# A third weight grid, four patch places and the sums on GpSimd's queue in a deformable sampling stage

## The reference

```python
def _dcnv3_core(x, offset, mask):           # B, H, W, C, G = 4, 56, 56, 128, 16; K = 9; GC = 8
    px = gx + dx + off[..., 0]              # places of the nine taps
    py = gy + dy + off[..., 1]
    x0, y0 = floor(pxf), floor(pyf)
    for cx, cy in ((x0, y0), (x0 + 1, y0), (x0, y0 + 1), (x0 + 1, y0 + 1)):
        wgt = (1 - abs(pxf - cx)) * (1 - abs(pyf - cy))
        v = take_along_axis(xg, idx, axis=1)
        acc = acc + (wgt * valid)[..., None] * v
    out = (acc * mask).reshape(B, H * W, K, G, GC).sum(axis=2)
```

## Time and profile before

| | |
|---|---|
| median of three runs | 3215.72 us |
| profiled execution, its own time | 3216.21 us |
| its span | 3214.5 us |
| VectorE busy, whole span | 2227.2 us (69%) |
| TensorE busy, whole span | 2288.7 us (71%) |
| clearing of the grids on GpSimd | 64 memsets, 187.1 us in all, mean 2.92 us |
| loads of `deform_xw` | 112 of 504 KB |
| loads and stores of `deform_yt` | 4 and 4, of 1568 KB each, median 7.2 us to landing |

### The profile page before, as it was taken

The page is one execution under the profiler, slowest core; times in us unless marked ns, Lnnn a source line. Parts: engine busy times, 40 slices in busy tenths (PEclk is TensorE's granted clock), DMA queues, the critical chain, the costliest instruction groups (busy, mean ns, idle before and its releaser), DMA issues. The chain is left out here.

```text
span 3214.5 us, 46923 instructions
## 1 busy us (share of the span) xinstructions
PE 2288.7 (71%) x15979; PEld 1511.7 (47%) x15979; DVE 2227.2 (69%) x4935; ACT 1623.1 (50%) x3184; POOL 1042.7 (32%) x1059
## 2 busy tenths in 40 slices
PE   5999804655756656527749999999999994403996
PEld 3555403555655555414415455455445553401775
DVE  2888846889899898439957768767777755400776
ACT  1444326667676676224456755664764631101664
POOL 0455501222122222139912222222122222273555
PEclk9999956877778778667769999999999995556998
DMA  6477748657657453462230002001001003012221
GB/s 180 100 182 162 179 115 220 172 148 197 174 144 186 139 147 88 107 258 80 79 82 1 1 1 60 1 1 37 24 1 31 11 10 104 5 41 90 90 90 52
DMA packets 343238, 304.60 MB, mean 95 GB/s; under 512 B 73775, under 2 KB 299703, under 8 KB 341536
## 3 DMA queue, kind: packets, MB, share of 16 engines
q1 hardware_dynamic: 334208, 294.00, 33.3%
q0 software_dynamic: 8800, 7.70, 0.8%
HBM read 158.50 MB, written 156.80 MB: 98 GB/s over the span
## 5 line engine op out<-in xcount | busy, mean ns | idle before, releaser
L1913 ACT ACTIVATE attn_prob<-attn_ps_e,attn_nm 128x448 f32<-128x448 f32 (+1 forms) x700 | 438.7, 632 | 324.5 <-DVE attn_nm L2000 321.9
L1817 PE MATMUL attn_ps_r<-attn_prob,attn_xs 128*128 128x448 f32 (+1 forms) x1400 | 585.7, 548 | 5.0 <-POOL attn_xs L1719 5.0
L940 PE MATMUL deform_ps_w<-all_ident,deform_grid 128*126 128x128 f32 x1568 | 268.0, 337 | 316.3 <-DVE deform_grid L1025 199.9
L2000 DVE TENSOR_REDUCE attn_nm<-attn_ps_e 128x1 f32<-128x448 f32 (+1 forms) x700 | 407.7, 615 | 36.7 <-PE attn_ps_e L1805 34.7
L866 POOL MEMSET deform_grid<- 128x3752 f32 (+1 forms) x64 | 187.1, 2924 | 709.1 <-PE deform_ps_w L940 663.4
L1716 POOL TENSOR_TENSOR attn_xs<-attn_xa,attn_wz 128x381 f32<-128x381 f32 (+1 forms) x200 | 184.4, 946 | 715.8 <-DVE attn_wz L2021 715.8
L940 PEld LDWEIGHTS deform_ps_w<-all_ident,deform_grid 128*126 128x126 f32 x1568 | 231.6, 176 | 351.5 <-DVE deform_grid L1025 211.3
L1817 PEld LDWEIGHTS attn_ps_r<-attn_prob,attn_xs 128*128 128x128 f32 (+1 forms) x1400 | 263.5, 192 | 208.2 <-issue 176.8
L900 ACT ACTIVATE deform_wt<-deform_ps_w 126x896 f32<-126x896 f32 x224 | 203.5, 933 | 227.5 <-PE deform_ps_w L940 143.1
L885 ACT ACTIVATE deform_hat<-deform_rel,block_negr 128x504 f32<-128x504 f32 (+1 forms) x256 | 258.6, 1124 | 104.0 <-DVE deform_rel L985 103.7
L1025 DVE TENSOR_TENSOR deform_grid<-deform_grid,deform_prod 128x448 f32 (+1 forms) x512 | 297.8, 582 | 8.8 <-DVE deform_grid L1025 7.9
(11 more groups left out here) (321 smaller groups left out, 4131.1 us busy)
## 6 DMA issues: line engine op xcount, KB each, us to landing
deform_xw<-shifted SPq DMA_DIRECT2D x112, 504.0 KB
shifted<-deform_xm SPq DMA_DIRECT2D x8, 4032.0 KB, 12.4
offsets_masks<-offs_om SPq DMA_DIRECT2D x48, 378.0 KB
deform_om<-offsets_masks SPq DMA_DIRECT2D x48, 378.0 KB
dispatched<-rows_zero SPq DMA_DIRECT2D x1, 16512.0 KB, 48.7
experts_bi<-dispatched SPq DMA_DIRECT2D x32, 516.0 KB, 3.5
deform_xa<-projected SPq DMA_DIRECT2D x64, 168.0 KB
projected<-offs_zero SPq DMA_DIRECT2D x13, 680.0 KB
```

What stands on the lines that cost most here:

```text
L940: mm = pe.transpose(ps_w[n % 2][0:NPOS, q * LANES:(q + 1) * LANES], grid[:, u % 2, at:at + NPOS], ident[:, :])
L1817: mm = pe.matmul(ps_r[n % 2][:, 0:BK], xs[0:rows, at + i, j, :], prob[0:rows, at + i, j * BK:(j + 1) * BK], start=(i == 0), stop=(i == len ...
L1913: nc.scalar.activation(prob[0:rows, slab(S) + i, ch * BK:(ch + 1) * BK], ps_e[u % NE][0:rows, 0:BK], ACT.Exp, bias=nm[0:rows, S % 2, i, ch ...
L2000: nc.vector.tensor_reduce(nm[0:rows, S % 2, i, ch:ch + 1], ps_e[u % NE][0:rows, 0:BK], AX, ALU.max, negate=True).then_inc(mx_ok, 1)
```

## The change

Three edits, all in the sampling stage.
1. `grid` has three places instead of two; GpSimd clears the grid of unit u once unit u-3 has been transposed.
2. `xw` has four places instead of eight, one window. The loads of a phase's first window are issued at its third unit, those of its second window at the first unit of the next phase; before, they were issued at its second and third unit.
3. The load and the store of `yt` go from SP's list to GpSimd's, and stand there between memsets.

```diff
-NOM, NCHUNK = 3, 8
+NOM, NCHUNK, NGRID = 3, 4, 3
...
             store_mixed(0)
             load_shifted(2)
-            load_sums(0)
             for u in range(NU):
...
-                if 1 <= pos <= len(PHASES[phase]):
-                    load_windows(quad * NSUB + PHASES[phase][pos - 1])
+                if pos == 2:
+                    load_windows(quad * NSUB + PHASES[phase][0])
+                if pos == 0 and phase:
+                    load_windows(quad * NSUB + PHASES[phase - 1][1])
...
+        @block.gpsimd
+        def _(pool):
+            def load_sums(quad):
+                if quad:
+                    pool.wait_ge(yt_st, 16 * quad)
+                pool.dma_start(yt[:, :], yt_d[quad * 128:(quad + 1) * 128, :]).then_inc(yt_in, 16)
+            def store_sums(quad):
+                pool.wait_ge(sum_ok, NSTEP * NSUB * (quad + 1))
+                pool.dma_start(yt_d[quad * 128:(quad + 1) * 128, :], yt[:, :]).then_inc(yt_st, 16)
+            for u in range(NU):
+                if u >= NGRID:
+                    pool.wait_ge(turned, turns_before(u - NGRID + 1))
+                pool.memset(grid[:, u % NGRID, 0:len(unit_of(u)[1]) * SUB_STEP], 0.0).then_inc(blank, 1)
+                if u == 2:
+                    load_sums(0)
+                quad, r = divmod(u, NPH * GQ)
                 if quad and r == 3:
                     store_sums(quad - 1)
                     load_sums(quad)
             store_sums(NQD - 1)
-            sp.wait_ge(yt_st, 16 * NQD)
-
-        @block.gpsimd
-        def _(pool):
-            for u in range(NU):
-                if u >= 2:
-                    pool.wait_ge(turned, turns_before(u - 1))
-                pool.memset(grid[:, u % 2, 0:len(unit_of(u)[1]) * SUB_STEP], 0.0).then_inc(blank, 1)
+            pool.wait_ge(yt_st, 16 * NQD)
...
-                t.sb("grid", [LANES, 2, GRID_LEN]), t.sb("wt", [128, 2, GQ, SPX, LANES]),
+                t.sb("grid", [LANES, NGRID, GRID_LEN]), t.sb("wt", [128, 2, GQ, SPX, LANES]),
```

More of the change, by code:

```diff
@@ L819, in load_windows @@
                     sp.dma_start(xw[0:NPOS, c % NCHUNK, :, :], src).then_inc(xw_in[c % NCHUNK], 16)
[L821 to L828, removed]
             load_om(0)
@@ L939, in turn @@
                             at = window_at(y, i * SX + side, SX * len(unit_of(u)[1]))
-                            mm = pe.transpose(ps_w[n % 2][0:NPOS, q * LANES:(q + 1) * LANES], grid[:, u % 2, at:at + NPOS],
+                            mm = pe.transpose(ps_w[n % 2][0:NPOS, q * LANES:(q + 1) * LANES], grid[:, u % NGRID, at:at + NPOS],
                                               ident[:, :])
@@ L976, in region @@
                                     max_val=(GRID - R) * (WCOLS + 1), skip_runtime_bounds_check_because=why)
-                return bass.AP(grid, (u % 2) * GRID_LEN + at,
-                               [[2 * GRID_LEN, LANES], [STEP, SPX * len(subs)], [WCOLS, R], [1, R]])
+                return bass.AP(grid, (u % NGRID) * GRID_LEN + at,
+                               [[NGRID * GRID_LEN, LANES], [STEP, SPX * len(subs)], [WCOLS, R], [1, R]])
             def relative(u):
```

## The result

The changed kernel takes 3168.53 us (median of 4 runs, 3167.7 to 3171.89) against 3214.36 us for the kernel before (4 runs of the same comparison, 3212.9 to 3220.93). The ratio is 0.9855, with a 95% interval of 0.9838 to 0.9873: 1.45% faster. The forecast was 3161, with a range of 3140 to 3188. The profiled execution took 3168.29 us with a span of 3166.6.

The account below looks back on a forecast made before the run. VectorE, busy 730 of 865 us, was taken to bound the sampling stage, so only its idle time could be won. 16.3 + 14.6 + 20.0 + 5.2 - 1.5 = 54.6 us, giving 3161 us, range 3140 to 3188.

Parts of the forecast that it names:

- Third grid: VectorE's waits for GpSimd's grid clearing: gains of 14.6 us in phase 1, 20.0 in phase 2, 5.2 in the last quad.
- Start: Sampling stage's start: offsets of units 3 and 5 land earlier through SP's new order, gaining 16.3 us, bounds 5 to 25.4.
- Four window places: Window loads in the sampling stage: pieces still land before TensorE wants them, cost 0.
- Phase 3: Half-size last phase of quads 0 to 2: no grid wait lies in its chain, so gain 0.
- Rival (c): Start gains 5 us, not 16, or windows and om late in phase 3 by 2 to 3 each: 3173 to 3180; 14%.
- End: Last store of the sums, from GpSimd, at the stage's end: costs 1.5 us, bounds 0 to 6.
- (a): ScalarE's late hats eat all the steady gain of phases 1 and 2: 3196 us; 8%.
- (b): All 70.3 us of waits for cleared grids go, phase 3 included: 3131 us; 7%.
- (d): Slower: GpSimd's store of the sums is slow and blocks memsets; 3252 us if landing takes 40 us; 3%.
- (e): The edits cancel or change nothing measurable; 3%.
- What was to be seen: Signs: relative(5) near 514, om wait near 20 us, memset wait near zero, hats wait up 25, stage end near 1268.

Follow-up runs that it names:

- e2b_order4: The changed kernel with two grids instead of three, still four window places: 3208.81 us, ratio 0.9977 to the kernel before.
- e7_sums_sp: The changed kernel with the load and store of the sums back on SP's queue: 3166.36 us, ratio 0.9852 to the kernel before.
- e2_order: The changed kernel with two grids instead of three and eight window places instead of four: 3222.59 us, ratio 1.0011 to the kernel before.
- e4_om4: The changed kernel with four buffers for offsets instead of three, om(3) loaded with the first three: 3160.08 us, ratio 0.9817 to the kernel before.

## Why the prediction was right, and where it was not

Faster, inside the range, 7.5 us over the figure. Point by point:

- **Third grid**: right, and by its mechanism. 36.1 us in phases 0 to 2 against 34.6, of which 0.86 is a wait for the offsets of unit 6, at 542.76, that I had not counted; 5.8 against 5.2 in the last quad. ScalarE's new waits were read off the old trace to 0.2 us. e2b_order4 against the changed kernel gives 39 against 39.8.
- **Start**: 14.4 of 16.3. The `xs` store landed 12.5 us after its issue (502.89 to 515.39), where 11.8 had been read from the earlier trace rows, and the first offsets landed 0.7 us later than my sharing of bytes gave. The part for moving `yt` off SP's queue is borne out: 3.9 us at relative(3), where e7_sums_sp gives 4.0 and the forecast had 4.6.
- **The step that failed**: "Four window places ... Cost 0", and with it "Phase 3: here I expect nothing in three quads". It was mis-sized: 8.4 us were lost, three times in phase 3. I had asked whether the pieces land in time, and they do (the stops follow the count of matmuls and not the pieces). I had not asked what else uses the DMA engines while they land. The new order puts two windows and the offsets into phase 3, where the old one put one window, so loads are still in flight while TensorE samples window 5. TensorE's next block of instructions comes through busy DMA engines and is late. The forecast had laid the risk on the four places; e2_order, with eight, stops too. TensorE lies on the chain there, as the forecast itself said: sample 5, transposes, hats(16). Without the stops phase 3 would have gained up to 0.9 us a quad (42.1 for 42.98).
- **Rival (c)** priced "windows and om late in phase 3 by 2 to 3 us each", and the size was near, but that was luck, since the reason was another: om(16) was 2.9 us late and cost nothing (e4_om4), and no stop inside a window was for a late piece.
- **End**: 1.0 us against 1.5; a plain DMA holds GpSimd 0.54 us, where the forecast had gone by an indirect one's 0.98. **Rivals (a), (b), (d), (e)** fell; GpSimd's stores landed in 5.4 to 8.9 us, where 31 was the point of break-even.
- **What was to be seen**: the wait for `hats` was to rise by some 25 us and did by more than that; the wait for offsets was to be near 20 and was 32.8: the forecast's own terms leave 39.9 - 16.3 = 23.6, and I left out three waits in phase 3 (8.5 us, off the path).

## What to carry to other kernels

When loads are issued at other places of the program, they move under other work. Ask not only whether they land in time, but what the engine then running must fetch through the same DMA engines, its own instructions included, and whether that engine is on the chain there. When a wait goes, read from the old trace which engine's queue is late next: here its order was worth three quarters as much (0.9855 to 0.9763) as the third grid (0.9977 to 0.9855). And read an edit's worth where it acts: the sums' move was worth 4 us there and nothing over the program, since TensorE's stops fell elsewhere.

## What the runs showed of the hardware

- TensorE's instructions come in packets of 16.4 KB for about 127 matmuls with their weight loads, and where TensorE stopped inside a window it went on 1.25 to 1.71 us after one had landed. At a DMA share near 1 (load of windows) crossing into the next block cost up to 3.8 us, but not every time: of 68 packets in the changed kernel's stage four came with such a stop. With the same loads cut to an eighth (share 0.13 to 0.66) it cost nothing inside window 5. The Trainium skill (Runtime: NRT & Kernel Launch, "Instruction fetch mechanics") says that an engine's instructions are fetched in 16 KiB blocks of 256 by a DMA queue of its own, and that the crossing is mostly hidden. The trace agrees with the block; the runs show when it is not hidden.
- In the list of waits such a stop has no releaser ("issue"), and the same word stands for TensorE's wait for VectorE's gather (6 us ahead of a whole window). A run cut at a fixed count, as x128 or x172 of 256, tells the one from the other.
- GpSimd issued a plain DMA of the sums in 0.54 us, and it landed in 8.7 us (median) from GpSimd, against 7.2 from SP.
